# Edge attention of a two-layer graph network: weights and decays stored as factors, one division at the end, key and radial products as tiles of the array, merged vector steps, longer runs of q and of the sums

## The reference, cut to what matters

```python
q = (x @ Wq).reshape(n, 8, 8);  x_src = x[src]
def conv(edge_attr, edge_sh, Wang, Wlin, W1, b1, W2):
    rad = relu(edge_attr @ W1 + b1) @ W2
    return (x_src * (edge_sh @ Wang.T)) @ Wlin * rad
k = conv(... key weights ...)      # 64 values an edge
v = conv(... value weights ...)    # 128 values an edge
alpha   = einsum(q[dst], Wdot, k)  # 8 heads
ealpha  = exp(alpha - segment_max(alpha, dst)[dst])
attn    = ealpha / segment_sum(ealpha, dst)[dst]
out     = segment_sum(attn * v, dst) @ Wout
x = layernorm(x + out)
```

## Time and profile before

| | us |
|---|---|
| median of three runs | 5307.28 |
| the profiled execution: time, span | 5309.66, 5307.9 |
| adjacency, 0 to 600 | 600 |
| hops, 600 to 2250 | 1650 |
| first node layer and q, to the start of attention | about 240 |
| attention, first gather to last store | 2504.2 to about 5139 |
| last gather, last node layer | to 5307.9 |

### The profile page before, as it was taken

How to read it: one execution, slowest core, us unless ns; L and a number is a source line. 1 busy time by engine, 2 the same in 40 slices (tenths; PEclk the granted TensorE clock), 3 DMA queues, 4 the chain that set the end, 5 groups by cost and what they waited for, 6 DMA issues and landing times. The chain is left out here.

```text
span 5307.9 us, 66619 instructions
## 1 busy us (share of the span) xinstructions
PE 4432.0 (83%) x19382; PEld 2894.7 (55%) x19382; DVE 3888.6 (73%) x6001; ACT 2422.2 (46%) x3740; POOL 2022.3 (38%) x1942
## 2 busy tenths in 40 slices
PE   4666689899999999741999999999999999999823
PEld 4666577777777777630445445544544454544412
DVE  7999654545545454441689999999998999999945
ACT  5666555554545545330444444444444444444411
POOL 3333000000000000015766666666666666766422
PEclk9888899999999999855999999999999999999955
DMA  3333699998999989403599999999999999999961
GB/s 109 103 103 101 143 221 219 197 229 184 222 193 222 227 182 232 83 0 79 140 230 249 256 246 257 249 247 254 254 246 241 251 248 244 256 247 241 241 179 35
DMA packets 1847237, 1043.13 MB, mean 197 GB/s; under 512 B 1316550, under 2 KB 1666372, under 8 KB 1846892
## 3 DMA queue, kind: packets, MB, share of 16 engines
q1 hardware_dynamic: 1441835, 700.05, 59.8%
q10 hardware_dynamic: 344208, 211.90, 13.7%
q0 software_dynamic: 60848, 127.02, 9.1%
HBM read 763.53 MB, written 274.94 MB: 196 GB/s over the span
## 5 line engine op out<-in xcount | busy, mean ns | idle before, releaser
L2076 POOL DMA_INDIRECT e_x_rows<-x_table,e_src x1616 | 1682.5, 1041 | 824.5 <-issue 438.9
L1144 PE MATMUL acc<-t_wide,scaled 128*128 128x512 f32 (+1 forms) x6370 | 1466.2, 388 | 120.5 <-DVE t_wide L1281 75.6
L1144 PEld LDWEIGHTS acc<-t_wide,scaled 128*128 128x128 f32 x6370 | 1165.7, 191 | 406.9 <-ACT t_wide L1162 137.6
L1162 ACT CAST t_wide<-t_ring 128x1176 fp32r<-128x1176 uint8 (+1 forms) x490 | 597.0, 1255 | 303.1 <-PE acc L1144 212.9
L1281 DVE CAST t_wide<-t_ring 128x1764 fp32r<-128x1764 uint8 (+1 forms) x490 | 535.0, 1124 | 223.5 <-PE acc L1144 220.2
L1647 POOL MEMSET l_eps<- 128x1 f32 x2 | 0.2, 102 | 1648.3 <-POOLq L1347 1639.6
L2402 DVE TENSOR_TENSOR_SCAN e_vsum<-e_factors,e_vsum,e_weighted 128x512 f32<-128x512 f32 x403 | 519.2, 1288 | 14.2
L539 PE MATMUL lists_rows_ps<-lists_hot_lo,lists_hot_hi 128*128 128x196 fp8e4 x3200 | 377.4, 286 | 177.3 <-DVE lists_hot_hi L464 177.3
L2271 ACT COPY e_out_rows<-e_b_o 128x512 f32<-128x512 f32 x404 | 236.8, 586 | 564.4 <-PE e_b_o L2166 436.9
L2142 PE MATMUL e_b_lv<-e_x_gv,e_wlin_v 128*128 128x512 f32 x808 | 431.1, 615 | 72.6 <-DVE x_res L2366 38.2
L1291 DVE TENSOR_TENSOR e_less<-e_x,e_part 128x512 f32<-128x512 f32 x101 | 69.9, 692 | 548.9 <-ACT e_part L1184 336.6
(11 more groups left out here) (207 smaller groups left out, 6250.4 us busy)
## 6 DMA issues: line engine op xcount, KB each, us to landing
e_factors<-share_rows SPq DMA_DIRECT2D x404, 512.0 KB
sums_table<-e_out_rows ACTq DMA_DIRECT2D x404, 256.0 KB
t_ring<-adjacency_bytes SPq DMA_DIRECT2D x245, 416.5 KB, 6.2
t_ring<-adjacency_bytes SPq DMA_DIRECT2D x245, 367.5 KB, 4.8
q_first<-hop_zeros_q ACTq DMA_DIRECT2D x101, 512.0 KB, 4.5
e_q_rows<-q_first SPq DMA_DIRECT2D x404, 128.0 KB
e_same_dst<-same_row SPq DMA_DIRECT2D x404, 128.0 KB
adjacency_bytes<-lists_staged SPq DMA_DIRECT2D x196, 196.0 KB, 2.7
```

Of the source, the lines that this page charges most:

```text
L1144: mm = nc.tensor.matmul(acc[c][:, 0:n], U[p][:, b, :], flat_t[:, lo:lo + n], start=(b == 0 and p == 0), stop=(b == NB - 1 and p == 1), ski ...
L1162: nc.scalar.copy(wide[g % WIDE][:, h0:h1, :], ring[g % BYTES][:, h0:h1, :]).then_inc(wide_act, 1)
L2076: nc.gpsimd.indirect_dma_start(x_rows[g % 3][:, j, :], None, x1_table, bass.IndirectOffsetOnAxis(ap=src[:, g * GT + j:g * GT + j + 1], axis=0)
```

## The change

It touches `edge_attention`, the q part of `node_layer`, and `attention_output`.

1. **Weights and decays as factors, division at the end.** `invert` and `shares` go. The factors are now exp(score - maximum so far) and the decay exp(old maximum - new maximum), which step 4 has anyway; the scan over values is then an undivided sum. SyncE stores them in step 4, at the end of its iteration, by eight DMAs of 16 rows for each of the two factors (32 KB each), into a table laid out by pair: `[pair, factor, head, group, edge]`. The running sums of weights of each round are turned by TensorE (`turn_sums`, four transposes in the new step 7), copied and stored by ScalarE (`store_sums`). After the loop GpSimd gathers the sums at each node's last edge (49 indirect DMAs), VectorE inverts them (128 x 392) and multiplies by `has_edges`; `attention_output` multiplies by the result.
2. **Late step of a pair at a time, 14 iterations late instead of 16.** `weigh` and `add_up` work on 1024 columns; `weigh` stands early in VectorE's iteration and `add_up` after `queries`. Factors have 3 buffers of a pair (1 MB) instead of 5 of a group. The table of values, `vsum` and `weighted` follow.
3. **Array tiles.** `linear_k` becomes two products with 64 columns of weights, one to each half of the bank's partitions. The radial values of a pair's second group and `radial_k` become four products of 64 rows by 64 columns, one on each quarter of the array, at the place of `radial_k`.
4. **Merged steps.** Both gates of a group lie in two adjacent banks and are multiplied by x in one instruction of 1024 columns. `queries` is one scan of 512 columns without the copy.
5. **Longer runs.** `q_first` is laid out so that the rows of a pair's two groups alternate; one DMA loads a pair's q, 2 KB in one run for each partition, and TensorE writes the transposes at every fourth column. The sums leave as 2 KB runs (partition p holds edges 4p to 4p+3), and `turn_out` reads every fourth column. Five small integer steps compute the new rows in `node_layer`, five more in `edge_attention`.

```diff
+        value: LATE buffers of [D, 2 * GE];  factors: 3 x [P, 2, 2 * GE];  vsum: 2 x [P, 2 * GE]
-        share_rows = nc.dram_tensor("share_rows", [ROUNDS * P, 2, GE], ...)
+        share_rows = nc.dram_tensor("share_rows", [PAIRS, 2, H, 2, GE], ...)
+        total_rows = nc.dram_tensor("total_rows", [ROUNDS * P * GT * ROWS, H], ...)
             def load_pair(p):
-                for half in range(2):
-                    sp.dma_start(q_rows[s][:, :, half, :],
-                                 q_first[cols(2 * p + half), :].rearrange("(j p) q -> p j q", p=P)...
+                sp.dma_start(q_rows[s][:], q_pairs[cols(p), :].rearrange("(p j) q -> p j q", j=GT))...
             def store_shares(t):
-                sp.wait_ge(v_round, t * N_V + V_OWN)
-                sp.dma_start(rows[:, 0, :], weight[0:n, :]).then_inc(shares_out, 16)
-                sp.wait_ge(v_round, t * N_V + V_PAST)
-                sp.dma_start(rows[:, 1, :], c_past[0:n, :]).then_inc(shares_out, 16)
+                for k, rows, ready in ((0, weight, A_WEIGHT), (1, decay, A_DECAY)):
+                    sp.wait_ge(a_round, t * N_A + ready)
+                    for j in range(scores_done(t) - t * PER_ROUND):
+                        sp.dma_start(share_rows[t * PER_ROUND + j, k].rearrange("h g e -> g h e"),
+                                     rows[j * ROWS:(j + 1) * ROWS, :]).then_inc(shares_out, 16)
-            def load_factors(g):
+            def load_factors(p):
+                t, j = divmod(p, PER_ROUND)
+                if j == 0:
+                    sp.wait_ge(shares_out, 32 * scores_done(t))
+                if p >= FACTORS:
+                    sp.wait_ge(v_sum, p - FACTORS + 1)
+                for k in range(2):
+                    sp.dma_start(factors[p % FACTORS][:, k, :],
+                                 share_rows[p, k].rearrange("h g e -> h (g e)").unsqueeze(0).to_broadcast(...)
             for i in range(LAST):
-                (store_shares, load_factors, load_pair, load_round)
+                if late(i + 1) is not None:
+                    load_factors(late(i + 1))
+                if i + 2 < PAIRS:
+                    load_pair(i + 2)
+                (load_round of step -4)
+                t = round_at(i, AT_WEIGHT)
+                if t is not None:
+                    store_shares(t)
+            (GpSimd, after its loop)
+            pool.wait_ge(sums_out, 16 * ROUNDS)
+            for b in range(NB):
+                nc.gpsimd.indirect_dma_start(sums_last[:, b, :], None, total_rows,
+                    bass.IndirectOffsetOnAxis(ap=sums_at[:, b:b + 1], axis=0)).then_inc(sums_got, 16)
+            def radial(p):
+                for half in range(2):
+                    at = slice(half * DQ, (half + 1) * DQ)
+                    nc.tensor.matmul(b_r[at, :], w2v[HID:2 * HID, at], hidden[1][HID:2 * HID, :], ...)
+                    nc.tensor.matmul(b_k[at, :], w2k[:], hidden[half][0:HID, :], ...)
             def linear_k(p):
                 for half in range(2):
-                    mm = nc.tensor.matmul(b_k[:], wlin_k[:, (1 - half) * DQ:(1 - half) * DQ + P],
-                                          x_gk[(2 * p + half) % 4][:], start=(half == 0), stop=(half == 1))
+                    nc.tensor.matmul(b_k[half * DQ:(half + 1) * DQ, :], wlin_k[:], x_g[(2 * p + half) % 4][:, 0, :], ...)
             (VectorE's loop)
                 gated(2 * i); lifted
-                shares;  weigh(g0);  add_up(g0)
+                weigh(late(i))
                 values; products; gated(2 * i + 1); queries; round steps
-                weigh(g1);  add_up(g1)
+                add_up(late(i))
                 values; local_top / whole_top, drop / local_weights / whole_weights
-                invert
```

More of the change, by code:

```diff
@@ L2184, in hand_out, with turn_sums @@
                                  stop=True).then_inc(p_small, 1)
+            def turn_sums(t, turned):
+                n = groups_of(t) * H
+                by_run = local[0:n, :].rearrange("r (p j) -> r j p", j=GT)
+                pe.wait_ge(v_round, t * N_V + V_WSUM)
+                if turned > 0:
+                    pe.wait_ge(a_out, turned)
+                for j in range(GT):
+                    tr = nc.tensor.transpose(b_o[:, j * P:j * P + n], by_run[:, j, :], ident[0:n, 0:n])
+                tr.then_inc(p_small, 1)
             for i in range(LAST):
                 now, last = i < PAIRS, 1 <= i <= PAIRS
-                first_out, second_out = turned_at(i)
-                turned = min(max(2 * (i - LATE), 0), G)
+                done = late(i - 1)
+                turned = 0 if i <= LATE else 2 * min(i - 1 - LATE, PAIRS) + (done is not None)
                 if now:
@@ L2202, in _ @@
                 if now:
-                    radial_v(2 * i)
+                    radial_v(i)
                     gate(2 * i + 1)
@@ L2226, in _ @@
                     linear_v(2 * i - 1)
+                    gather_scores(i - 1)
                 if now:
-                    radial_v(2 * i + 1)
-                if last:
-                    gather_scores(i - 1)
-                for t, step in read_by:
-                    pe.wait_ge(v_round, t * N_V + step)
-                if second_out is not None:
-                    turn_out(second_out)
-                if now:
-                    radial_k(i)
+                    radial(i)
+                for read, count in read_by:
+                    pe.wait_ge(read, count)
+                if done is not None:
+                    turn_out(2 * done + 1)
         @block.scalar
@@ L2306, in _ @@
                     hide(2 * i)
-                if first_out is not None:
-                    store(first_out)
+                if done is not None:
+                    store(2 * done)
                 if now:
@@ L2518, in _ @@
                     lifted(at_weight)
-                if at_share is not None:
-                    shares(at_share)
-                if late(i):
-                    weigh(late(i)[0])
-                    add_up(late(i)[0])
+                if late(i) is not None:
+                    weigh(late(i))
                 if last:
@@ L2537, in _ @@
                     take_weights(at_sum)
-                if late(i):
-                    weigh(late(i)[1])
-                    add_up(late(i)[1])
+                if late(i) is not None:
+                    add_up(late(i))
                 if last:
```

351 lines of the change are left out of this document (186 added, 165 removed).

## The result

The changed kernel takes 5471.91 us (median of 4 runs, 5424.87 to 5477.01), the kernel of before 5305.36 in the same session: ratio 1.0295, 95% interval 1.0263 to 1.0327. It is slower by 3%. The forecast was 5320 in a range of 5130 to 5480: the time lies inside, near the upper end. The profiled execution took 5477.01 us, its span 5475.0.

The account below looks back on a forecast made before the run. TensorE, VectorE and the DMA engines were taken as close to full, TensorE and VectorE alternating. Rounds -31 and end +44 on the profiled 5309.7 us gave +13, 5323, less 2.4 for the median: 5320, range 5130 to 5480.

Parts of the forecast that it names:

- the likeliest case: Attention rounds lose their gain to a stall on two-engine stores; 5320 us, own range 5240 to 5400, chance 0.50.
- Stores of weights and decays: Once a round, stores through two DMA engines at 48 GB/s make VectorE wait 10 us for factors, 5 to 13.
- A round without the stall: Eight attention pairs, without waiting for the stores, were to take 88 to 89 us.
- the DMA engines and GpSimd both now floor light pairs at about 10.7: In attention's light pairs these two were to set about 10.7 us a pair, above VectorE's 9.4.
- Merged vector steps, no reciprocal: VectorE in attention: 0.68 us less a pair, so 9.4; a round 84 us, 10 less than now.
- Array tiles: TensorE's key and radial products partly overlap, 0.86 us saved, 10.5 a pair; bounds 2.6 saved to 0.86 dearer.
- The rival without overlap: TensorE's tiles don't run beside each other: 12.2 us of TensorE a pair, about 5508 us, chance 0.16.
- draining: Rival: each change of tile shape exposes about 0.16 us of TensorE, four times a pair; 5362 us, chance 0.12.
- Longer runs and the first pairs: Longer DMA packets for sums and q save 0.7 us a pair, 0 to 1.1; first 14 pairs at 10.4 us.
- Start and end: Outside the rounds: -16 us after the last pair, +60 for 49 gathers of sums; end +44.
- what was to show it right: Profile signs: stores under 60 GB/s, weighing waiting 5 to 13 us, other pairs 10 to 11, 61 us of gathers.
- the tiles' 1.3 and 2.2 us: Profile sign on TensorE: `linear_k` at about 1.3 us, the four radial products at 2.2 from start to start.

Follow-up runs that it names:

- the best version: Changed kernel with weights and decays stored by row, four row buffers, the sums' scan in halves and two stores a round: 5111.33 us, ratio to before 0.9636.
- the 5161 us kernel: Changed kernel with weights and decays stored by row, four row buffers and the scan of the sums in halves: 5161.23 us, ratio to before 0.9731.
- the fourth buffer: Four instead of three buffers for gathered x rows, added to the changed kernel with stores by row: 5291.07 us, ratio to before 0.9978.

## Why the prediction was right, and by how much it missed

The mechanism named for the likeliest case came: the gain in the rounds goes into a stall at the first factors, and the end pays for gathers. But the sum was +13 us and the result +167; two terms of the rounds were mis-sized, by some 150 us together. That 5472 still lies inside 5130 to 5480 is in part luck: the likeliest case's own range ended at 5400, and the room above it was kept for tiles that don't run beside each other, which they do.

- **Stores of weights and decays.** Right in place, once a round, and in cause: with 16 rows as the outermost dimension on both sides the stall shrinks by 8 us, and the queue moved 43 GB/s where 48 was forecast. Size: 13.5 us measured, 10 taken, the range ended at 13. +3.5 us a round, some 80 us. The Trainium skill's rule cited in the forecast ("DMA: Bandwidth & Descriptors", Why a DMA increments its semaphore by 16 and not by 1) agrees with this.
- **A round without the stall.** 88 to 89 forecast, 105.4 - 13.5 = 91.9 measured: +3 us, some 70 us. The step that failed is "the DMA engines and GpSimd both now floor light pairs at about 10.7": GpSimd's 10.8 us a pair was taken from gathers of 1.047 us, as if a property of GpSimd, but it depends on the VectorE step that runs beside it, and the change doubled that step. 8 x (1.181 + 0.30) = 11.85 us a pair. The DMA engines, at 0.87, were not the floor; whether they are at the 1.00 of the best version no run tells.
- **Merged vector steps, no reciprocal.** VectorE needs 82.5 us a round, 84 forecast. No run undid all of it; the one merge that was undone, the scan of the sums, gave VectorE more to do and took 102 and 130 us off.
- **Array tiles.** Forecast 1.29 and 2.15 us from a reading between the bounds; measured 1.01 and 1.02, near full overlap. The rival without overlap (5508) gave almost the right time for a wrong reason; only the rows tell them apart. A group costs 0.09 us before it and 0.15 to 0.16 after it beyond its two passes, 0.5 us a pair where the forecast priced draining at 0.64. No run here tells a drain at the change of mode (the Trainium skill, "TensorEngine Tiling (Array Packing)", Key Properties) from another fixed cost; either way it is 0.5 us a pair against the 2.6 saved in passes. Without the tiles the 5161 us kernel loses 101.
- **Longer runs and the first pairs.** The first twelve pairs, which have no late step, go at (2640.1 - 2518.3) / 12 = 10.15 us against (2650.3 - 2522.4) / 12 = 10.66, faster than the 10.4 forecast and close to 8 x (0.944 + 0.30) = 9.95, GpSimd's need when no scan of sums meets it. The transposes were taken as free: those of the sums cost 0.3 us a pair more, those of q still 0.44 us for four (3991.21 to 3991.65). What the runs of q and output give by themselves wasn't tried. The once-a-pair line in that window, changed kernel, then the kernel of before:

```profile
L2443 DVE TENSOR_TENSOR_SCAN e_q_t<-e_same_dst,e_b_x x13: 1203/1209/1211, 2518.3 to 2640.1; 128x512 f32<-128x512 f32 x13
```

```profile
L2384 DVE COPY e_q_t<-e_b_x x13: 141/145/158, 2522.4 to 2650.3; 128x1 f32<-128x1 f32 x13
```

- **Start and end.** +44 forecast, -4.1 + 49.7 = +45.6 measured; the gathers of sums 61 us, and 64 to 70 without them.

Of what was to show it right, the stall (half a microsecond beyond its 5 to 13), the slow stores, the gathers and pairs of 10 to 11 us came; the tiles' 1.3 and 2.2 us did not. The pair of 15 to 20 us that waits for gathered rows was not on the list.

## What to carry to other kernels

When an engine is relieved, ask again which engine runs without a pause, and take its step's time from rows with the new neighbour in mind: a gather from GpSimd waits out a long VectorE step whose inputs both lie in SBUF, so where GpSimd sets the pace two short steps are better than one long. Give both sides of a DMA an outermost dimension that sixteen engines can share, and look at the stored layout before adding buffers or moving issues: here it was worth 170 us, and the fourth buffer on top of it nothing clear of noise.

## What the runs showed of the hardware

- A gather that starts inside a scan with both inputs in SBUF takes 2.38 us in the mean, inside one that reads PSUM 0.944. One that started before the scan isn't held.
- Four 64x64 tiles in fp32, two passes each, take 1.02 us to the start of what follows; two 128x64 tiles with 512 columns 1.01. What stands before such a group is followed 0.09 us later than its own passes take.
- Four transposes that read every fourth column take 0.58 us, with columns side by side 0.44.
- 512 KB in 16 stores with an outermost dimension of 2 hold SyncE 7.5 us a round, and move at 43 GB/s, 1.8 engines' worth of packet time; with 16 rows they hold it 1.5.
- After some 12 us without work TensorE restarts at a granted 0.50 and is at 1.00 ten microseconds later, so a stall costs more than its length.
- The same kernel of before took 5302 to 5306 us in three sessions and 5633 in one: differences of a per cent need a control beside them.
